# Second layer of a four-layer graph network: gathered groups spread to the last quarter step, six early chunks, roots behind the last block, merged comparisons in the build

## The reference, cut to what matters

```python
h = relu(layernorm(x)); x = x + light_gcn(h)      # 3 hops: sums of h[src] * dinv[src] * dinv[dst]; mean of the 4 states
h = relu(layernorm(x)); x = x + relu(gcn_conv(h, edge_weight, W, b))
h = relu(layernorm(x)); x = x + (h @ W_self.T + mean_over_edges(h[src]) @ W_neigh.T)
h = relu(layernorm(x)); x = x + node_update(h, edge_mlp(h[src], h[dst], edge_attr_64))

def gcn_conv(x, edge_index, w, W, b):              # layer 2 (self edges with weight 1 are appended)
    deg = segment_sum(w, col)
    dinv = where(deg > 0, rsqrt(deg), 0)
    msg = (x @ W)[row] * (dinv[row] * w * dinv[col])[:, None]
    return segment_sum(msg, col) + b
```

## Time and profile before

| | |
|---|---|
| median of three runs | 1041.11 us (1039.91 to 1047.62) |
| profiled execution, its own time | 1044.67 us |
| span of the profiled execution | 1042.8 us |
| PE busy | 909.4 us (87%) |
| VectorE (DVE) busy | 807.8 us (77%) |
| GpSimd (POOL) busy | 558.6 us (54%) |
| ScalarE (ACT) busy | 440.8 us (42%) |
| mean granted clock of TensorE | 0.946 |

### The profile page before, as it was taken

How to read it: one execution, slowest core, us unless ns; L and a number is a source line. 1 busy time by engine, 2 the same in 40 slices (tenths; PEclk the granted TensorE clock), 3 DMA queues, 4 the chain that set the end, 5 groups by cost and what they waited for, 6 DMA issues and landing times.

```text
span 1042.8 us, 24302 instructions
## 1 busy us (share of the span) xinstructions
PE 909.4 (87%) x6245; PEld 587.0 (56%) x6245; DVE 807.8 (77%) x2574; ACT 440.8 (42%) x876; POOL 558.6 (54%) x728
## 2 busy tenths in 40 slices
PE   2788887999948988888789579999999999999995
PEld 2566664455436767676546445555555555555553
DVE  8999998534677768888767767777778777787786
ACT  3687875011035555555302424444443444444441
POOL 6434452000037777777000367777777777777770
PEclk9699997999979989899899789999999999999997
DMA  3111124400032222222080465454444444444541
GB/s 68 42 50 50 60 97 172 181 1 1 1 78 76 65 67 67 67 66 68 12 277 5 95 166 116 106 110 108 104 100 105 104 107 103 101 105 104 108 88 34
DMA packets 153882, 89.62 MB, mean 86 GB/s; under 512 B 112493, under 2 KB 137274, under 8 KB 153690
## 3 DMA queue, kind: packets, MB, share of 16 engines
q1 hardware_dynamic: 137016, 72.81, 25.6%
q0 software_dynamic: 15424, 15.83, 8.5%
q10 hardware_dynamic: 1378, 0.22, 0.1%
HBM read 67.52 MB, written 21.27 MB: 85 GB/s over the span
## 4 chain that ended last, share of the span: by engine, by line
PE 46%; DVE 25%; POOL 12%; issue 11%; DVEq 3%; DMA 3%; ACT 0%; SPq 0%; ACTq 0%
PE seg L1704 10%; POOL pair L1272 9%; PE seg L1889 6%; PE big L1925 6%; PE big L1915 3%; PE seg L1936 3%; PE seg L1628 3%; PE seg L1957 3%; POOL A L1272 2%; DVE A L2050 2%; DVE acc_mem L2248 2%; PE big L1628 2%; DVE A L2150 2%; PE seg L1946 1%; DVE A L2154 1%
## 5 line engine op out<-in xcount | busy, mean ns | idle before, releaser
L1272 POOL DMA_INDIRECT A<-table,src_i x338 | 321.3, 951 | 117.1 <-issue 96.0
L1272 POOL DMA_INDIRECT pair<-table,src_i x144 | 148.6, 1032 | 57.0 <-issue 43.6
L1889 PE MATMUL seg<-A 128*128 128x384 f16 (+1 forms) x624 | 121.4, 338 | 10.7 <-DVE A L2116 8.2
L1748 PE MATMUL big<-A 128*128 128x300 bf16 (+1 forms) x544 | 100.9, 331 | 19.0 <-DVE A L2039 14.1
L1925 PE MATMUL big<-A 128*128 128x512 f32 x208 | 109.8, 610 | 2.9 <-DMA A<-pr_table 2.9
L1543 ACT ACTIVATE A<-big,A 128x512 f32<-128x512 f32 x104 | 71.5, 687 | 94.6 <-PE big L1926 94.6
L1537 ACT COPY A<-big 128x512 f32<-128x512 f32 x104 | 60.7, 584 | 119.9 <-PE big L1915 119.7
L1889 PEld LDWEIGHTS seg<-A 128*128 128x128 f16 x624 | 57.4, 99 | 90.0 <-issue 35.2
L1472 ACT COPY A<-big 128x500 f32<-128x500 f32 x136 | 74.8, 570 | 47.1 <-PE big L1748 46.3
L1748 PEld LDWEIGHTS big<-A 128*128 128x128 f16 x544 | 69.2, 148 | 36.5 <-DVE A L2039 15.6
L2150 DVE TENSOR_TENSOR A<-seg,A 128x448 f32<-128x448 f32 x78 | 48.7, 625 | 50.6 <-PE seg L1892 29.7
(11 more groups left out here) (333 smaller groups left out, 1728.9 us busy)
## 6 DMA issues: line engine op xcount, KB each, us to landing
A<-in_edge_attr_dram SPq DMA_DIRECT2D x103, 128.0 KB, 2.3
A<-drel_flat SPq DMA_DIRECT2D x104, 126.0 KB
A<-lanes_kept SPq DMA_DIRECT2D x34, 256.0 KB
spilled_adjacency<-A SPq DMA_DIRECT2D x1, 7074.0 KB, 21.9
A<-spilled_adjacency SPq DMA_DIRECT2D x6, 1152.0 KB, 10.6
A<-table,src_i POOLq DMA_INDIRECT x338
lanes_kept<-acc_mem SPq DMA_DIRECT2D x17, 256.0 KB
lanes_kept<-xs SPq DMA_DIRECT2D x17, 256.0 KB, 2.1
```

What stands on the lines that cost most here:

```text
L1272: pool.indirect_dma_start(out=row, out_offset=None, in_=table, in_offset=bass.IndirectOffsetOnAxis(ap=src_i[:, tile:tile + 1], axis=0)).th ...
L1748: op = nc.tensor.matmul(pair_window(k)[:, :, low:high], hot_l1[:, h, m, :, (2 * k + j) % 8], sub_hots(hot_r1, 2 * (k % 4) + j, high - low) ...
L1889: op = nc.tensor.matmul(made[:, 0:held.shape[2] * D], hot_low[:, u, m, :], held[:, k, :, :], start=(m == 0 and k == 0), stop=(m == 3 and k ...
```

## The change

It has four parts.

1. `sum_step` spreads the 36 gathered groups over steps 4 to 67 in place of 4 to 63.
2. `early_pairs` has eight blocks in place of nine. With the later groups, six gathered chunks (0 to 5) and the weighted chunks 9 to 16 are early; chunks 6 and 17 move into the first `conv1_late` and its `late_nodes`, six chunks in place of four. The two columns 6 and 17 thus need no separate subtraction ahead of `late_nodes`.
3. `roots1`, the subtraction and the scaling of the ready chunks move from behind block 15 to behind block 16, ahead of the trailing additions (`block_step(NB, q)`).
4. In the build, the two halves of a round are compared by one instruction each for lanes and columns (`both_same_as`, 2048 and 200 columns). The waits of both halves stand ahead of the first comparison, and the semaphore for PE (`lanes_ready`) rises by two behind the second.

```diff
-EARLY_WEIGHTED = tuple(range(SIDE, SIDE + 9))
+EARLY_WEIGHTED = tuple(range(SIDE, SIDE + 8))
...
 def sum_step(g):
-    return g + Q + 6 * Q * g // (Q * IT1 - 1)
+    return g + Q + 7 * Q * g // (Q * IT1 - 1)
...
     # early_pairs()
-    assert c == 7
+    assert c == 6
...
-assert max(EARLY_AT) == NB - 3
+assert max(EARLY_AT) == NB - 4
...
+        hot_b2 = [m.rearrange("p (h v k) -> p h v k", h=2, k=4) for m in
+                  (small[:, PAIRS:PAIRS + 2 * NC * 4], xs_h[:, 2 * 8 * P:2 * 8 * P + 2 * NC * 4])]
+        hot_l2 = [m.rearrange("p (h v k) -> p h v k", h=2, k=8) for m in (acc_h[:, hot_l_at:keys_at], xs_h[:, 0:2 * 8 * P])]
...
             pe.wait_ge(acc_step, Q + SUMS1 - PS)
-            conv1_late(LATE_BANKS[0], (7, 8, LATE_STRIDE + 7, LATE_STRIDE + 8))
+            conv1_late(LATE_BANKS[0], (6, 7, 8, LATE_STRIDE + 6, LATE_STRIDE + 7, LATE_STRIDE + 8))
...
+            def both_same_as(out_, keys, lanes, wide):
+                return dve.tensor_tensor(out_, keys.rearrange("p h (a k) -> p h a k", a=1).broadcast_to([P, 2, lanes, wide]),
+                                         iota_8[:, 0:lanes, 0:wide].rearrange("p (h a) k -> p h a k", h=1).broadcast_to([P, 2, lanes, wide]),
+                                         ALU.is_equal)
...
             # window_hots(it, degrees, odd, turn, first_kept=0)
-                for half in range(2):
-                    h = 2 * odd + half
-                    if turn >= 2:
-                        dve.wait_ge(window_built, it * PS + (half + 1))
-                        if half:
-                            dve.wait_ge(lanes_moved[h], it * 8 - 8 * odd)
-                        elif first_kept:
-                            dve.wait_ge(lanes_moved[h], it * 8 - 8 * (odd + first_kept))
-                    same_as(hot_l[h], key_l[:, bass.ds(it * PS + half * 2 * CUT, 8)], P, 8)
-                    same_as(hot_b[h], key_b[:, bass.ds(it * STREAM + half * CUT, 4)], NC, 4).then_inc(lanes_ready, 1)
+                if turn >= 2:
+                    dve.wait_ge(window_built, it * PS + 2)
+                    dve.wait_ge(lanes_moved[2 * odd + 1], it * 8 - 8 * odd)
+                    if first_kept:
+                        dve.wait_ge(lanes_moved[2 * odd], it * 8 - 8 * (odd + first_kept))
+                both_same_as(hot_l2[odd], key_l.rearrange("p (h c) -> p h c", h=2)[:, :, bass.ds(it * PS, 8)], P, 8)
+                both_same_as(hot_b2[odd], key_b.rearrange("p (h c) -> p h c", h=2)[:, :, bass.ds(it * STREAM, 4)], NC, 4).then_inc(lanes_ready, 2)
...
             # the order of DVE's program from block 1 on
-                if b == NB - 2:
+                if b == NB - 1:
                     roots1()
                     for cols, _ in sides:
                         link(dve.tensor_tensor(hs[:, cols, :], xs[:, cols, :], per_node(mean1)[:, cols, :], ALU.subtract))
                         scaled(cols)
...
             def both_late(v):
-                return of_both(v, 7, 9)
+                return of_both(v, 6, 9)
...
-            link(dve.tensor_tensor(of_both(hs, 6, 7), of_both(xs, 6, 7), of_both(per_node(mean1), 6, 7), ALU.subtract))
             dve.wait_ge(ev("conv1_out"), 1)
-            late_nodes(big[:, LATE_BANKS[0], 0:4 * D].rearrange("p (k c d) -> p k c d", k=2, d=D), both_late,
-                       spare(4).rearrange("p (k c) d -> p k c d", k=2))
+            late_nodes(big[:, LATE_BANKS[0], 0:6 * D].rearrange("p (k c d) -> p k c d", k=2, d=D), both_late,
+                       spare(6).rearrange("p (k c) d -> p k c d", k=2))
```

## The result

| | before | changed |
|---|---|---|
| median | 1041.9 us (4 runs, 1039.91 to 1047.62) | 1031.58 us (4 runs, 1026.78 to 1032.43) |
| ratio to before | 1 | 0.9883, 95% interval 0.9856 to 0.9910 |
| span of the profiled execution | 1042.8 us | 1030.1 us |
| DVE busy | 807.8 us | 799.9 us |
| PE busy | 909.4 us | 907.2 us |

The account below looks back on a forecast made before the run. DVE was taken to bound the build, the gather layer 2 until 398.7 us, then DVE with the gather close behind. Build 3.5 plus layers 2 and 3 13.3 (17.7 - 4.4) gave 16.8 us, forecast 1024.5 us, range 1018 to 1034.

Parts of the forecast that it names:

- a sign of being wrong: Layer 2: the prediction would be wrong if DVE never waited for PE after group 16.
- build, to the first gather: Build: two merged comparisons in place of four save 0.14 us a round, 3.5 us over 26 rounds.
- step 67, from the first gather: End of layer 2: PE's last step starts at 500.4 in place of 518.11 us, a gain of 17.7 us.
- way behind step 67: Layer 2 into layer 3: DVE's chain to layer 3's late sums ends 4.4 us later, counted from step 67.
- DVE without a gap: Build: one round takes 5.46 us on DVE without a gap, so time taken from DVE's round shortens the kernel.
- one run of early nodes would be absorbed ahead of group 16: Layer 2: one of eight early runs, 2.5 us, falls before 398.7 us, in time that DVE idled away.
- the 2.5 us that I had added for mutual waits: Layer 2, up to step 67: gather and DVE limits meet, so 2.5 us of waits move 497.9 to 500.4.
- the rival in which DVE drags: Layer 2: without DVE's lead step 67 starts at 505, the tail may cost 6.6 us; 1031 us, chance 0.15.
- The term of 3.7 us: Behind step 67: roots 5.2, additions and comparison 0.8, less 2.25 of cover, delay the additions releasing the late projection.
- PE at half clock: Layer 3's first sums: PE at 1.2 GHz after stands, up to 10 us more, some 8 beyond slack; 1032, chance 0.08.
- Nothing gained outside the build: Steps 64 to 67: their gain is all lost again behind them, only 3.5 us remain, 1037.6 us; chance 0.05.
- one column a cycle: Every build round: merged comparisons run at half speed, +1.0 us a round, 26 us, 1054 us; chance 0.06.

Follow-up runs that it names:

- waits in front: Kernel before, its four comparisons of a build round kept, with the waits of both halves in front of the first; 1043.28 us in one run.
- merge only: Kernel before with only the two merged comparisons of the build; 1041.74 us against 1042.61, ratio 0.9990 (0.9972 to 1.0007).
- the two runs with more work on DVE: Changed kernel with extra DVE passes, in one run behind group 16 (1039.94 us), in the other ahead of it (1036.20 us).
- changed kernel again: The changed kernel measured a second time, nothing altered; 1029.84 us, ratio 0.9879 to the kernel before.
- roots back: Changed kernel with the roots behind block 15 again, all else as changed; 1035.20 us, ratio 0.9934 (0.9917 to 0.9951).
- grouped, addition first: Changed kernel with early nodes in four DVE runs, centred rows written to `hs`, and group 34's addition ahead of the roots; 1029.37 us, ratio 0.9877.
- more DVE work: Changed kernel with the squares of the early nodes made five times in place of once; 1039.94 us in one run.
- roots only: Kernel before with the roots moved behind block 16 and nothing else; 1041.67 us against 1042.61, ratio 0.9992 (0.9980 to 1.0003).

## Why the prediction was right, and where its sizes were off

The direction and the range held, and so did the mechanism in its main parts: faster by over 1%, out of the build and out of the end of layer 2, with a part given back by the roots. One thing that the prediction had called a sign of being wrong came as well: DVE never waited for PE between group 16 and the last step. The gain was 12 us by the ratio (10 by the two medians) where 16.8 were forecast. By its terms:

| term | forecast | the two profiles | means over executions |
|---|---|---|---|
| build, to the first gather | -3.5 | -1.9 | -2.7 |
| step 67, from the first gather | -17.7 | -15.9 | -14.3 |
| way behind step 67 | +4.4 | +6.0 | +6.0 |
| behind the late sums | 0 | -0.9 | not told from zero |
| sum | -16.8 | -12.7 | -11.0 |

The means are over nine kernels with merged comparisons and three without for the first line, over three executions of the changed kernel and three with the old order (before, waits in front, merge only) for the others.

**Build.** The round was right to the hundredth. What was missing is the start: the shorter rounds reach PE in rounds 3 and 4, and stand there 0.3 to 0.8 us. In the profiled execution the 0.55 us for POOL came on top. "DVE without a gap" had been read from one round in the middle.

**Step 67.** Three things were off. First, the base: in the profiled execution of before PE ran at half pace behind a stand at step 43 (PE's timeline):

```profile
431.11 1.41 PE L1748 MATMUL big<-A 128*128 128x300 bf16 x8
...
436.09 0.66 PE L1786 MATMUL seg<-pair 128*64 128x42 f32 x8 [2.61 <-ACT pair L1481]
436.69 2.56 PE L1748 MATMUL big<-A 128*128 128x300 bf16 x8
```

Its step 67 came 2.4 to 2.7 us later than in the two other executions with the same layer 2. Merge only has the same stand there with a shorter slow stretch, waits in front has none; at step 63 the execution of before was 1.6 us behind both, and the rest came in the slow stretch behind the stand of 6.32 us. A gain counted from that execution was too large by about 1.7 us against the mean of the three. Second, the claim that one run of early nodes would be absorbed ahead of group 16, because DVE is two steps further on: that is the step that failed. All eight runs lie behind it, the first one barely (in the kernel before it stood 7.5 us behind), as DVE's timeline of the changed kernel shows:

```profile
398.02 0.29 DVE L2085 TENSOR_TENSOR pair<-seg,dinv 128x128 f32<-128x128 f32 x1
```

It starts 0.8 us after the sum of group 16 (397.23). Third, the 2.5 us that I had added for mutual waits were no waits: DVE never waited for PE there. They stood for the run that was not absorbed, the right size for the wrong reason. That these two cancel is luck. What is left of the miss, 197.3 against 195.4, is 0.8 us up to group 16's sum (94.2 for 93.4) and 1.1 from there to step 67 (103.1 us for 500.4 - 398.4 = 102.0).

So the rival in which DVE drags was right in its mechanism (no lead, no absorption), which the two runs with more work on DVE show directly, and partly right in its price. It had step 67 at 505 - 305.0 = 200.0, a figure that the prediction does not work out and that lies above its own bound of 504.2; the measured 197.3 lies between this and the forecast. Its tail of 6.6 us is near the measured 6.0, but for another reason than its own: the roots did find cover, and the next paragraph has what cost the rest.

**The way behind step 67.** The term of 3.7 us up to the first pair additions measured 508.21 - 500.32 less 520.63 - 518.11, 5.4. Roots 5.2 as forecast; the cover 1.9 in place of 2.25, since DVE reached the roots 0.6 us behind the start of step 67; and the two group additions, costed at a quarter of a group of four with the comparison at 0.8, took 2.06 us from 506.15 to 508.21. Their work is 0.4 us, the rest are three stands of 0.56, 0.71 and 0.39 us. A row of four additions shares one register load and one such stand; each single addition has its own, and the prediction had no term for it. The late nodes (+0.9) and the dropped subtraction (-0.3) were right.

**PE at half clock.** It came, as the rival said, and cost nothing here. The stand before the late projections was 4.40 us, not 2.3, and the matmuls behind it took 2.82 and 2.49 us; the clock granted from 500.3 to 530.6 was 0.89. But the late sums still waited for DVE's split (1.20 us), so the slack that the prediction named held. In the changed kernel again the slow stretch was longer and that wait was down to 0.87 us, still there. Where PE's slow stretch lies in front of work on which DVE waits (roots back), it is paid.

**Nothing gained outside the build** and **one column a cycle** are out by the lines above.

## What to carry to other kernels

A duration read from a full row of like instructions is a throughput; where an instruction stands alone in a chain, what its engine's queue does ahead of it can be the larger part (0.2 us of work, 0.9 us in all, 0.32 of it a register load), so when work is moved to the end of a stage, count its single instructions with their loads and waits. When a bound is moved from one engine to another, adding and taking away a known amount of work on each side of the suspected turning point (here +9.8 us behind and +7.9 ahead of group 16, with 11.7 and about 1 us seen) tells where the bound changes better than any busy share. And a base taken from one execution carries that execution's accidents: read the stage from two or three before a gain is promised in it.

## What had not been expected of the hardware

One small operation of POOL can be held up through many operations of DVE. In the build of the changed kernel (timeline of POOL, then of DVE):

```profile
86.00 5.18 POOL L1331 TENSOR_TENSOR pair<-pair,chunk_start 128x6 f16 x4 [1.27 <-DVE cur L2260]
...
97.27 0.96 POOL L1331 TENSOR_TENSOR pair<-pair,chunk_start 128x6 f16 x4 [1.91 <-DVE cur L2260]
```

```profile
87.07 1.21 DVE L2233 TENSOR_TENSOR xs<-acc_mem,iota 128x2048 f16<-128x2048 f16 x1
88.21 0.25 DVE L2233 TENSOR_TENSOR xs<-pair,iota 128x200 f16<-128x200 f16 x1
88.38 2.29 DVE L2254 TENSOR_SCALAR acc_mem<-iota_r,acc_mem 128x300 f16<-128x300 f16 x10
91.22 0.56 DVE L2260 TENSOR_TENSOR cur<-pair,cur 128x768 f16<-128x768 f16 x1 [0.55 <-POOL pair L1331]
```

Four operations of 128x6 elements take under 1 us in 11 of the 25 rounds, 2.2 to 3.2 in others, and 5.18 here; one of them spans 4.72 us. It ended when DVE ran out of work and waited for it, behind sixteen operations of DVE that had all begun after it (two comparisons and fourteen hot columns). The kernel grouped, addition first, has the same 5.18 us in the same round, and waits in front 5.32 us in another. The Trainium skill (SBUF — State Buffer, SBUF: two separate sides) describes the ports that DVE and GpSimd share as a lock that the one who starts first holds for its whole instruction, where DVE's operation reads two inputs from SBUF or uses two ports. The trace agrees with a lock, and shows besides that the one who waits may be passed over by instruction after instruction. That it is this lock is inferred from the times; no run here took the ports apart.

Stands of PE of very different length were followed by half pace. Behind 6.32 and 6.40 us of idle time the next eight matmuls took 2.52 us in place of 1.41, and behind 2.67 us (more DVE work) 2.55, at a granted clock of 0.50 (498.4 to 500.9). Behind 1.30 us (roots only, step 67) they took the usual 1.41.
